# Turning the values of the looped head groups on VectorE instead of TensorE, and sharing out the closing sums

## The chip, the cores and the metric

The kernel runs on one core of a Trainium2 chip. The metric is the device time of one execution in microseconds, the median of several runs. Engine names are those of the profile: PE is TensorE (PEld its weight loads), DVE is VectorE, ACT is ScalarE, POOL is GpSimd, SP issues the DMAs.

## The reference

One decoder block on x of 8 sequences with 128 rows and 512 columns, in three residual steps:

```python
x = x + attn(layernorm(x))            # 32 query heads, 8 key/value heads of 128, causal softmax
x = x + cross(ctx, ctx, layernorm(x)) # sim = ctx @ query^T * scale, softmax, @ ctx
x = x + ffn(layernorm(x))             # 4-bit weights, 512 -> 1376 -> 512
...
q = (hidden_states @ w_q).reshape(B, S, Hkv, g, D)
k = (hidden_states @ w_k).reshape(B, S, Hkv, D)
v = (hidden_states @ w_v).reshape(B, S, Hkv, D)
...
attn = jnp.einsum('bhgqk,bkhd->bqhgd', probs, v)
return attn.reshape(B, S, Hq * D) @ w_o
...
inter = gate * jax.nn.sigmoid(gate) * up
out = (inter @ Wd).astype(jnp.float16)
```

## The kernel before

Most matmuls are done in three passes on numbers that are split into a high and a low part (`_hi`, `_lo`), so each product is `hi*hi + hi*lo + lo*hi` (`passes`, L495 to L498). ScalarE usually makes the high part by rounding, VectorE or GpSimd the low part by subtraction.

Self attention goes over 8 groups of heads (g), one key/value head with its 4 query heads each. Seven of them run in a hardware loop (`group(g)` of every engine), the eighth (`last_group`) is written out and mixed with the cross attention. A pass of the loop is cut into slots t; the work of every engine is written out slot by slot, and the engines meet only through semaphores. Sequence u (8 of them) has its scores in slot t = u (`scores`, L627), its mask, maximum and exponentials there too, the transposition of its probabilities (`turn_probs`, VectorE, ten blocks of 32x32 for 4 heads at once, L1413) in slot u + 1, the product with the values (`values(g, u)`, into one PSUM bank) in slot u + 2, the output projection (`out_heads(g, u)`) in slot u + 3, and its addition to the residual (`add_heads`, VectorE, L1403) in slot u + 4. Between them TensorE projects the next keys, values and queries: `FILL` says which of the 12 blocks (key, value, four query blocks, each for two halves of the batch) is projected in which slot, 12 matmuls each. The second half (n = 1) is that of this group, the first half (n = 0) that of the next group. ScalarE empties every block (`fill_out`, into `qt`, `kt` or `vt`).

The projected values come out with the head's 128 elements on the partitions, and `values` wants the keys there. So `turn_values` of TensorE transposes them in four pieces of 128x128 behind the first fill of slots 2 (n = 1) and 6 (n = 0) into the PSUM bank `BK_VT` (`turn_v`, L516); ScalarE rounds them there to `v_hi` (`values_first`, L837), VectorE subtracts to `v_lo` (`values_second`, L1373).

GpSimd has, for every sequence, the normalisation of the probabilities (L1164) and `pt_lo` (L1175), and the low parts of the weights (L1149). VectorE also unpacks 4-bit weights in four steps a pass (`unpack_step`, L1422 and L1427, in slots 0, 0, 9 and 10).

The feed forward part ends with eight products of the last row tile (`down_half`, two halves h of the rows, four column pieces j, each into a bank of its own). Piece j = 0 of each half is scaled by ScalarE (L1086) and added by GpSimd (L1246), pieces 1 to 3 are done by VectorE in one instruction (`last_sums`, L1639). TensorE transposes the sums of sequences 0 to 3, then 4 to 7 (L811); VectorE adds them to the residual (`last_adds`, L1646) but for those in `Y_POOL`, which ScalarE copies (L1090) and GpSimd adds (L1250); SP stores the 8 tiles in order (L485).

Of the kernel before, what the change touches and what calls it, by code (L numbers as in the profile page):

```python
# [17 lines left out]
P = 128  # L18
# [7 lines left out]
def decoder_kernel(nc, x, ctx_in, ctx_turned, w_q, w_k, w_v, w_o,  # L26
# [21 lines left out]
    TURN_V = {2: 1, 6: 0}  # L48
# [31 lines left out]
    with ExitStack() as stack:  # L80
# [56 lines left out]
        with ExitStack() as scope:  # L137
            sb = allocator(scope)
            xt_hi = sb("xt_hi", [P, HC, T], F32R)
            xt_lo = sb("xt_lo", [P, HC, T], F32R)  # L140
            wq_hi = sb("wq_hi", [P, HG, HC, P], F32R)
            wq_lo = sb("wq_lo", [P, HG, HC, P], F32R)
            wk_hi = sb("wk_hi", [P, HC, P], F32R)
            wk_lo = sb("wk_lo", [P, HC, P], F32R)
            wv_hi = sb("wv_hi", [P, HC, P], F32R)
            wv_lo = sb("wv_lo", [P, HC, P], F32R)
            wq_raw = sb("wq_raw", [P, HC, HG * P])
            wk_raw = sb("wk_raw", [P, HC, P])
            wv_raw = sb("wv_raw", [P, HC, P])
            wo_raw = sb("wo_raw", [P, HG, H])  # L150
            wo_hi = sb("wo_hi", [P, HG, H], F32R)
            wo_lo = sb("wo_lo", [P, HG, H], F32R)
            qt = sb("qt", [P, HG, T])
            kt = sb("kt", [P, T])
            vt = sb("vt", [P, HALF])
            v_hi = sb("v_hi", [P, NB, P], F32R)
            v_lo = sb("v_lo", [P, NB, P], F32R)
            probs = sb("probs", [P, 2, HG, P])
            pt = sb("pt", [P, HG, P])
            pt_hi = sb("pt_hi", [P, HG, P], F32R)  # L160
# [58 lines left out]
        vt_done = sem("vt_done")  # L219
        vt_hi = sem("vt_hi")  # L220
# [110 lines left out]
        Y_POOL = (2, 5)  # L331
# [158 lines left out]
        def _(pe):  # L490
# [23 lines left out]
            def turn_v():  # L514
                for k in range(BH):
                    mm = pe.transpose(psum[:, BK_VT, k * P:(k + 1) * P], vt[:, k * P:(k + 1) * P], ident[:])  # L516
# [48 lines left out]
            turn_v()  # L565
# [66 lines left out]
            def turn_values(g, n):  # L632
# [3 lines left out]
                turn_v()  # L636
# [180 lines left out]
        def _(act):  # L817
# [9 lines left out]
            def project_out(unit, n, bank):  # L827

                cols = slice(n * HALF, (n + 1) * HALF)
                dst = vt[:] if unit == "v" else kt[:, cols] if unit == "k" else qt[:, int(unit[1:]), cols]  # L830
# [92 lines left out]
            def values_first(g, n):  # L923

                act.wait_ge(vt_done, g * NH + (3 - n))
                act.wait_ge(pv_done, g * NB + (0 if n == 1 else BH) + PRIME)
                v_first(n)

            def fill_out(g, i):
# [3 lines left out]
                if unit == "v":  # L933
                    act.wait_ge(vt_done, g * NH + (2 - n))
# [24 lines left out]
            def group(g):  # L959
                step = g * NB  # L960
                for t in range(SLOTS):
                    if t < NB:
                        exponentials(g, t)
                    for k, i in enumerate(FILL.get(t, ())):
                        fill_out(g, i)
                        if k == 0 and t in TURN_V:
                            values_first(g, TURN_V[t])
# [115 lines left out]
            for h in range(NH):  # L1083
# [3 lines left out]
                        d_s[:, 0, NT - 1:NT]).then_inc(last_part, 1)  # L1087
            for i, b in enumerate(Y_POOL):
# [5 lines left out]
        def _(pool):  # L1094
# [73 lines left out]
            def group(g):  # L1168
                n = 0
                for t in range(SLOTS):  # L1170
# [71 lines left out]
            for h in range(NH):  # L1242
# [4 lines left out]
                                   ALU.add).then_inc(last_pool, 1)  # L1247
            for i, b in enumerate(Y_POOL):
# [5 lines left out]
        def _(dve):  # L1254
# [160 lines left out]

            def unpack_step(g, i):
# [60 lines left out]
            def group(g):  # L1477
                for t in range(SLOTS + 1):
# [12 lines left out]
                    if t in TURN_V:  # L1491
                        values_second(g, TURN_V[t])
# [4 lines left out]
                    if t in UNPACK:  # L1497
                        unpack_step(g, UNPACK[t])

# [150 lines left out]
            last_sums(1, (1,))  # L1650
            last_adds(0)
            last_sums(1, (2, 3))
# [38 lines left out]
```

## Time and profile before

| | |
|---|---|
| median of 3 runs | 733.5 us (733.18 to 734.48) |
| the profiled execution's own time | 734.44 us |
| its span | 732.5 us |
| TensorE busy | 713.0 us, 97% |
| VectorE busy | 563.0 us, 77% |
| ScalarE, GpSimd busy | 381.7 and 378.3 us, 52% each |
| TensorE clock granted over the span | 0.993 of full |
| DMA | 63.91 MB, 87 GB/s on average |

Busy time is the sum of the stretches in which an engine had an instruction. Matmuls are pipelined, and their ends are modelled: what one costs is read from the distance of the starts. Times in the rows below are us from the start of the span. One pass of the loop, from the scores of sequence 0 to the same in the next pass, takes some 68 us; the second of the seven goes from 99.7 to 167.7 us.

### The profile page before, as it was taken

To read this page: it belongs to the slowest core of one execution; us is meant where nothing else is said; L and a number is where in the kernel's file an instruction comes from. 1 tells how busy PE (TensorE), PEld (TensorE's weight loads), DVE (VectorE), ACT (ScalarE), POOL (GpSimd) and SP (SyncE) were. 2 spreads that over 40 slices of the span, in tenths; PEclk is the share of its full clock that TensorE was granted. 3 is DMA by queue.
4 is the path that set the end of the run, shared out by engine and by line. 5 is a ranking of instruction groups with operands and counts; after the bars stand their busy time and mean duration, and the time that the engine had idled before them with its cause. 6 is when DMAs were issued, how large, how long until landed. Compare 5 with 4: busy or idle time off the path is not lost.

```text
span 732.5 us, 11268 instructions
## 1 busy us (share of the span) xinstructions
PE 713.0 (97%) x3506; PEld 591.2 (81%) x3506; DVE 563.0 (77%) x1178; ACT 381.7 (52%) x965; POOL 378.3 (52%) x361
## 2 busy tenths in 40 slices
PE   8999999999999999999999999999999889999995
PEld 7888888888888888888888888888877657888873
DVE  6588768877886888688778867875378888888897
ACT  4575536535552654265346435652556556555552
POOL 4275426535542654264435525551445535788875
PEclk9999999999999999999999999999999999999997
DMA  9532046105701540361036003302900001321103
GB/s 303 163 84 91 2 125 210 38 0 144 230 0 38 175 152 0 97 190 38 0 115 200 0 9 99 142 0 73 334 10 2 0 4 55 86 82 41 30 12 115
DMA packets 44901, 63.91 MB, mean 87 GB/s; under 512 B 4462, under 2 KB 23278, under 8 KB 44878
## 3 DMA queue, kind: packets, MB, share of 16 engines
q1 hardware_dynamic: 44878, 63.62, 27.7%
q8 instruction: 12, 0.20, 0.1%
q14 instruction: 11, 0.09, 0.0%
HBM read 52.67 MB, written 10.95 MB: 87 GB/s over the span
## 4 chain that ended last, share of the span: by engine, by line
PE 87%; DVE 5%; POOL 3%; issue 2%; ACT 2%; DMA 0%; POOLq 0%; DVEq 0%; ACTq 0%
PE psum L496 21%; PE psum L498 21%; PE psum L497 21%; PE psum L627 7%; PE psum L715 5%; PE psum L716 5%; PE psum L738 2%; PE psum L737 2%; DVE stats L1267 1%; PE psum L516 1%; ACT probs L918 1%; PE psum L502 1%; POOL o_sum L1227 1%; DVE xprobs L1393 1%; DVE negmax L1458 0%
## 5 line engine op out<-in xcount | busy, mean ns | idle before, releaser
L1164 POOL TENSOR_TENSOR probs<-probs,rowinv 128x512 f32<-128x512 f32 x64 | 76.4, 1195 | 239.6 <-DVE rowinv L1464 239.6
L1413 DVE STREAM_TRANSPOSE pt<-probs 32x128 f32<-32x128 f32 x560 | 168.9, 302 | 13.9 <-POOL pt_lo L1175 7.1
L918 ACT ACTIVATE probs<-probs,negmax 128x128 f32<-128x128 f32 x256 | 99.8, 391 | 137.9 <-DVE negmax L1458 137.9
L496 PE MATMUL psum<-xt_hi,wq_hi 128*128 128x512 f32 x256 | 103.4, 404 | 0.0
L496 PE MATMUL psum<-wo_hi,at_hi 128*128 128x512 f32 x256 | 100.4, 392 | 0.5 <-DVE at_lo L1469 0.5
L498 PE MATMUL psum<-xt_hi,wq_lo 128*128 128x512 f32 x256 | 99.9, 390 | 0.0
L497 PE MATMUL psum<-xt_lo,wq_hi 128*128 128x512 f32 x256 | 99.8, 390 | 0.0
L498 PE MATMUL psum<-wo_hi,at_lo 128*128 128x512 f32 x256 | 99.7, 390 | 0.0
L497 PE MATMUL psum<-wo_lo,at_hi 128*128 128x512 f32 x256 | 99.6, 389 | 0.0
L1403 DVE TENSOR_TENSOR xacc<-psum,xacc 128x512 f32<-128x512 f32 x64 | 44.1, 690 | 64.5 <-PE psum L498 64.5
L1175 POOL TENSOR_TENSOR pt_lo<-pt,pt_hi 128x512 fp32r<-128x512 f32 x56 | 72.0, 1286 | 27.5 <-ACT pt_hi L974 27.5
L715 PE MATMUL psum<-ft_hi,gw 128*128 128x512 f32 (+1 forms) x176 | 71.2, 404 | 1.2 <-DVE ft_lo L1276 0.9
L627 PEld LDWEIGHTS psum<-kt,qt 128*128 128x128 f32 x512 | 66.8, 191 | 6.5 <-issue 1.4
L716 PE MATMUL psum<-ft_lo,gw 128*128 128x512 f32 (+1 forms) x176 | 69.7, 396 | 0.0
L832 ACT ACTIVATE qt<-psum 128x512 f32<-128x512 f32 x64 | 37.6, 588 | 59.6 <-PE psum L498 59.4
L627 PE MATMUL psum<-kt,qt 128*128 128x128 f32 x512 | 67.4, 274 | 0.3 <-ACT qt L832 0.3
L496 PEld LDWEIGHTS psum<-wo_hi,at_hi 128*128 128x128 f32 x256 | 48.1, 188 | 11.1 <-DVE at_lo L1469 1.2
L1454 DVE TENSOR_TENSOR probs<-psum,causal 128x512 f32<-128x512 f32 x64 | 44.2, 690 | 16.3 <-PE psum L627 16.1
L1469 DVE TENSOR_TENSOR at_lo<-psum,at_hi 128x512 fp32r<-128x512 f32 x64 | 43.2, 675 | 17.2 <-ACT at_hi L943 16.9
L498 PEld LDWEIGHTS psum<-xt_hi,wq_lo 128*128 128x128 f32 x256 | 48.0, 188 | 10.3
L498 PEld LDWEIGHTS psum<-wo_hi,at_lo 128*128 128x128 f32 x256 | 48.0, 188 | 10.2
L497 PEld LDWEIGHTS psum<-wo_lo,at_hi 128*128 128x128 f32 x256 | 48.1, 188 | 9.9
(153 smaller groups left out, 1530.8 us busy)
## 6 DMA issues: line engine op xcount, KB each, us to landing
wq_raw<-in_L_attn_w_q SPq DMA_DIRECT2D x8, 1024.0 KB, 5.6
wo_raw<-in_L_attn_w_o SPq DMA_DIRECT2D x8, 1024.0 KB, 7.8
u_zn<-zeros_gu SPq DMA_DIRECT2D x16, 344.0 KB, 6.4
unpacked_w<-u_q SPq DMA_DIRECT2D x8, 688.0 KB, 7.8
gw<-unpacked_w SPq DMA_DIRECT2D x20, 256.0 KB, 3.6
unpacked_w<-u_q SPq DMA_DIRECT2D x6, 512.0 KB, 6.7
u_q<-in_L_ffn_gate_qweight SPq DMA_DIRECT2D x8, 344.0 KB, 5.3
u_q<-in_L_ffn_up_qweight SPq DMA_DIRECT2D x8, 344.0 KB, 4.0
```

The source lines that it names most:

```text
L496: pe.matmul(dst, a_hi, b_hi, start=start, stop=False)
L497: pe.matmul(dst, a_hi, b_lo, start=False, stop=False)
L498: return pe.matmul(dst, a_lo, b_hi, start=False, stop=stop)
L627: mm = pe.matmul(psum[:, BK_S, j * P:(j + 1) * P], qt[:, j, t * P:(t + 1) * P], kt[:, t * P:(t + 1) * P], start=True, stop=True)
L715: pe.matmul(dst, gw[:, r, m, c, 0:w], ft_hi[:, c, cols], start=True, stop=False)
L716: return pe.matmul(dst, gw[:, r, m, c, 0:w], ft_lo[:, c, cols], start=False, stop=True)
L918: e = act.activation(probs[:, t % 2, j, :], probs[:, t % 2, j, :], ACT.Exp, bias=negmax[:, t % 2, j:j + 1], accum_out=rowsum[:, t % 2, j:j ...
L1164: pool.tensor_tensor(probs[:, t % 2], probs[:, t % 2], rowinv[:, t % 2, :].unsqueeze(2).to_broadcast([P, HG, P]), ALU.mult).then_inc(prob_ ...
L1175: pool.tensor_tensor(pt_lo[:], pt[:], pt_hi[:].bitcast(F32), ALU.subtract).then_inc(ptlo_ready, 1)
L1403: dve.tensor_tensor(xacc[:, u, :], psum[:, out_bank(g, u), :], xacc[:, u, :], ALU.add).then_inc(o_added, 1)
L1413: turned = dve.transpose(pt[keys, :, queries], probs[queries, t % 2, :, keys])
L1454: dve.tensor_tensor(probs[:, r], psum[:, BK_S, :].rearrange("p (a b) -> p a b", a=HG), causal[:].unsqueeze(1).to_broadcast([P, HG, P]), AL ...
```

## The change

The values of the looped groups are no longer transposed by TensorE. VectorE turns them in 16 blocks of 32 partitions for each half (`turn_values` there), one instruction for a block of four sequences, from `vt`, which now has a place for both halves, to a new tile `v_raw` in SBUF. `TURN_V` names the slots: half 1 in slots 1 to 4 with 4, 5, 4 and 3 blocks, half 0 in slots 8 to 10 with 4, 6 and 6. ScalarE rounds `v_raw` at the head of slots 5 and 11 (`values_rounded`), and the subtraction is now GpSimd's. The values ahead of the loop and those in the last group are turned as before.

In the closing part, the sum of piece 3 of the second half goes from VectorE to ScalarE and GpSimd; VectorE does its five sums ahead of all additions, and GpSimd's tiles are 3 and 6 in place of 2 and 5.

```diff
-    TURN_V = {2: 1, 6: 0}
+    TURN_V = {1: (1, 0, 4), 2: (1, 4, 9), 3: (1, 9, 13), 4: (1, 13, 16), 8: (0, 0, 4), 9: (0, 4, 10), 10: (0, 10, 16)}
+    SPLIT_V = {5: 1, 11: 0}
...
-            vt = sb("vt", [P, HALF])
+            vt = sb("vt", [P, 2, HALF])
+            v_raw = sb("v_raw", [P, BH, P])
...
-        Y_POOL = (2, 5)
+        Y_POOL = (3, 6)
...
# TensorE, group(g)
-                    for k, i in enumerate(FILL.get(t, ())):
+                    for i in FILL.get(t, ()):
                         fill(g, i)
-                        if k == 0 and t in TURN_V:
-                            turn_values(g, TURN_V[t])
...
             for b in range(NB):
-                pe.wait_ge(last_dve, (HC - 1) * (b // BH + 1))
-                pe.wait_ge(last_pool, b // BH + 1)
+                pe.wait_ge(last_dve, HC - 1 if b < BH else 2 * HC - 3)
+                pe.wait_ge(last_pool, 1 if b < BH else 3)
...
# ScalarE
+            def values_rounded(g, n):
+                act.wait_ge(v_turned, g * NH + (2 - n))
+                act.wait_ge(pv_done, g * NB + (0 if n == 1 else BH) + PRIME)
+                act.copy(v_hi[:, n * BH:(n + 1) * BH, :], v_raw[:]).then_inc(vt_hi, 1)
...
                 if unit == "v":
-                    act.wait_ge(vt_done, g * NH + (2 - n))
+                    act.wait_ge(vt_done, 1)
+                    act.wait_ge(v_turned, g * NH)
...
-                for t in range(SLOTS):
+                for t in range(SLOTS + 1):
+                    if t in SPLIT_V:
+                        values_rounded(g, SPLIT_V[t])
                     if t < NB:
                         exponentials(g, t)
...
+            act.wait_ge(last_done, NH * HC)
+            act.wait_ge(o_summed, SUMS_BEFORE + 2)
+            act.mul(o_part[:, 0, HALF:T], psum[:, NH * HC - 1, :], d_s[:, HC - 1, NT - 1:NT]).then_inc(last_part, 1)
...
# GpSimd
+                    if t in SPLIT_V:
+                        half = slice(SPLIT_V[t] * BH, (SPLIT_V[t] + 1) * BH)
+                        pool.wait_ge(vt_hi, g * NH + (3 - SPLIT_V[t]))
+                        pool.tensor_tensor(v_lo[:, half, :], v_raw[:], v_hi[:, half, :].bitcast(F32),
+                                           ALU.subtract).then_inc(vt_lo, 1)
...
+            pool.wait_ge(last_part, NH + 1)
+            done, count = copied(LAST_WINDOW, HC - 1)
+            pool.wait_ge(done, count)
+            pool.tensor_tensor(o16[:, HC - 1, HALF:T], o_part[:, 0, HALF:T], o_sum[:, HC - 1, HALF:T],
+                               ALU.add).then_inc(last_pool, 1)
...
# VectorE
+            def turn_values(g, n, first, last):
+                if first == 0:
+                    dve.wait_ge(proj_out, g * NBLK + FIRST_BLOCKS + BLOCKS.index(("v", n)) + 1)
+                    dve.wait_ge(vt_lo, g * NH + (2 - n))
+                for k in range(first, last):
+                    i, j = divmod(k, P // QUAD)
+                    heads, keys = slice(i * QUAD, (i + 1) * QUAD), slice(j * QUAD, (j + 1) * QUAD)
+                    turned = dve.transpose(v_raw[keys, :, heads],
+                                           vt[heads, n, :].rearrange("p (a b) -> p a b", a=BH)[:, :, keys])
+                if last == (P // QUAD) ** 2:
+                    turned.then_inc(v_turned, 1)
...
-                    if t in TURN_V:
-                        values_second(g, TURN_V[t])
                     if PV <= t < NB + 1:
                         heads_second(g, t - PV)
...
                     if t in UNPACK:
                         unpack_step(g, UNPACK[t])
+                    if t in TURN_V:
+                        turn_values(g, *TURN_V[t])
...
             last_sums(0, (1, 2, 3))
-            last_sums(1, (1,))
+            last_sums(1, (1, 2))
             last_adds(0)
-            last_sums(1, (2, 3))
             last_adds(1)
```

TensorE before, in slot 2: the end of its first fill, the four transposes of the values (`psum<-ident,vt`) and the start of the second fill.

```order
L497 MATMUL psum<-xt_lo,wq_hi 128x512
L498 MATMUL psum<-xt_hi,wq_lo 128x512
L635 ISA
L516 MATMUL psum<-ident,vt 128x128 x4
L643 REGISTER_ALU
L644 REGISTER_ALU
L496 MATMUL psum<-xt_hi,wq_hi 128x512
```

The same place in the changed kernel, whose lines are some three further down:

```order
L500 MATMUL psum<-xt_lo,wq_hi 128x512
L501 MATMUL psum<-xt_hi,wq_lo 128x512
L646 REGISTER_ALU
L647 REGISTER_ALU
L499 MATMUL psum<-xt_hi,wq_hi 128x512
```

The transposes and their wait are gone, and one block's matmuls follow the other's.

VectorE's row in slots 2 and 3 before, from mask(2) to the heads' subtraction of sequence 1 (`probs<-psum,causal` is the mask, `negmax` the maximum, `rowinv` the reciprocal, `at_lo` the subtraction of the heads, `v_lo` that of the values):

```order
L1454 TENSOR_TENSOR probs<-psum,causal 128x512
L1458 TENSOR_REDUCE negmax<-probs 128x4
L1413 STREAM_TRANSPOSE pt<-probs 32x4x32 x10
L1464 RECIPROCAL rowinv<-rowsum 128x4
L1474 ISA
L1373 TENSOR_TENSOR v_lo<-psum,v_hi 128x512
L1469 TENSOR_TENSOR at_lo<-psum,at_hi 128x512
L1453 REGISTER_ALU
L1454 TENSOR_TENSOR probs<-psum,causal 128x512
L1458 TENSOR_REDUCE negmax<-probs 128x4
L1413 STREAM_TRANSPOSE pt<-probs 32x4x32 x10
L1464 RECIPROCAL rowinv<-rowsum 128x4
```

The same place now, with the reciprocal of slot 1 and the first four blocks ahead of it:

```order
L1498 RECIPROCAL rowinv<-rowsum 128x4
L1440 ISA
L1441 ISA
L1445 STREAM_TRANSPOSE v_raw<-vt 32x4x32 x4
L1487 REGISTER_ALU
L1488 TENSOR_TENSOR probs<-psum,causal 128x512
L1492 TENSOR_REDUCE negmax<-probs 128x4
L1434 STREAM_TRANSPOSE pt<-probs 32x4x32 x10
L1498 RECIPROCAL rowinv<-rowsum 128x4
L1503 TENSOR_TENSOR at_lo<-psum,at_hi 128x512
L1445 STREAM_TRANSPOSE v_raw<-vt 32x4x32 x5
L1487 REGISTER_ALU
```

The subtraction of the values has left, and 4 and 5 block transposes stand at the ends of slots 1 and 2, ahead of the next slot's mask.

VectorE's last rows before:

```order
L1639 SCALAR_TENSOR_TENSOR o<-psum,d_s,o_sum 128x512 x4
L1646 TENSOR_TENSOR xacc<-psum,xacc 128x512 x3
L1639 SCALAR_TENSOR_TENSOR o<-psum,d_s,o_sum 128x512 x2
L1646 TENSOR_TENSOR xacc<-psum,xacc 128x512 x3
```

And now:

```order
L1673 SCALAR_TENSOR_TENSOR o<-psum,d_s,o_sum 128x512 x5
L1680 TENSOR_TENSOR xacc<-psum,xacc 128x512 x6
```

One sum has left, and none stands behind an addition any more.

## Rows read from the trace of the kernel before

**Rows 1.** The page: span, and busy time of each engine.
```profile
span 732.5 us, 11268 instructions
...
PE 713.0 (97%) x3506; PEld 591.2 (81%) x3506; DVE 563.0 (77%) x1178; ACT 381.7 (52%) x965; POOL 378.3 (52%) x361
```

**Rows 2.** Windows: second pass; length, busy PE, PEld, DVE, ACT, POOL, granted clock, DMA.
```profile
99.70:167.70 68.00, 68.00 (x337) 57.45 (x336) 52.40 (x126) 34.46 (x104) 32.27 (x26) 1.00 0.34 100
```

**Rows 3.** Waits of TensorE, whole span: us in total, times, longest.
```profile
PE psum L496 <- DVE at_lo L1469: 0.5, 1, 0.5
...
PE psum L627 <- ACT qt L832: 0.3, 1, 0.3
```

**Rows 4.** Timeline of TensorE, second pass: start, us, line, operation; score blocks, transposes.
```profile
103.28 1.05 PE L627 MATMUL psum<-kt,qt 128*128 128x128 f32 x8
...
109.63 1.05 PE L627 MATMUL psum<-kt,qt 128*128 128x128 f32 x8
...
113.26 0.60 PE L516 MATMUL psum<-ident,vt 128*128 128x128 f32 x4
...
117.12 1.05 PE L627 MATMUL psum<-kt,qt 128*128 128x128 f32 x8
...
131.18 1.05 PE L627 MATMUL psum<-kt,qt 128*128 128x128 f32 x8
...
138.20 1.05 PE L627 MATMUL psum<-kt,qt 128*128 128x128 f32 x8
...
145.72 0.49 PE L627 MATMUL psum<-kt,qt 128*128 128x128 f32 x3
```

**Rows 5.** Timeline of VectorE, slots 2 to 5; in brackets the idle time before.
```profile
112.74 3.14 DVE L1413 STREAM_TRANSPOSE pt<-probs 32x128 f32<-32x128 f32 x10 [0.61 <-POOL pt_lo L1175]
...
116.01 0.66 DVE L1373 TENSOR_TENSOR v_lo<-psum,v_hi 128x512 fp32r<-128x512 f32 x1
117.94 0.69 DVE L1469 TENSOR_TENSOR at_lo<-psum,at_hi 128x512 fp32r<-128x512 f32 x1 [1.27 <-ACT at_hi L943]
118.55 0.68 DVE L1454 TENSOR_TENSOR probs<-psum,causal 128x512 f32<-128x512 f32 x1
...
124.35 0.69 DVE L1403 TENSOR_TENSOR xacc<-psum,xacc 128x512 f32<-128x512 f32 x1 [0.51 <-PE psum L498]
125.24 0.69 DVE L1454 TENSOR_TENSOR probs<-psum,causal 128x512 f32<-128x512 f32 x1 [0.20 <-PE psum L627]
...
131.38 0.69 DVE L1403 TENSOR_TENSOR xacc<-psum,xacc 128x512 f32<-128x512 f32 x1 [0.88 <-PE psum L498]
```

**Rows 6.** Timeline of GpSimd, second pass: normalisation, weight splits, pt_lo.
```profile
104.14 2.44 POOL L1164 TENSOR_TENSOR probs<-probs,rowinv 128x512 f32<-128x512 f32 x1 [13.06 <-DVE rowinv L1464]
106.54 2.54 POOL L1149 TENSOR_TENSOR wo_lo<-wo_raw,wo_hi 128x512 fp32r<-128x512 f32 x2
...
131.00 1.27 POOL L1175 TENSOR_TENSOR pt_lo<-pt,pt_hi 128x512 fp32r<-128x512 f32 x1
```

**Rows 7.** Timeline of the closing part, all engines, from 719 us.
```profile
719.35 2.72 DVE L1639 SCALAR_TENSOR_TENSOR o<-psum,d_s,o_sum 128x512 f16<-128x512 f32 x4
...
720.55 2.49 POOL L1246 TENSOR_TENSOR o<-o_part,o_sum 128x512 f16<-128x512 f32 x2
...
721.96 1.48 PE L811 MATMUL psum<-ident,o 128*128 128x128 f16 x16 [1.28 <-POOL o L1246]
...
723.10 6.88 SPq L485 DMA_DIRECT2D out<-xacc  x8
...
725.64 1.89 PE L811 MATMUL psum<-ident,o 128*128 128x128 f16 x16 [2.20 <-DVE o L1639]
...
727.38 1.26 POOL L1250 TENSOR_TENSOR xacc<-y_part,xacc 128x512 f32<-128x512 f32 x1 [2.39 <-ACT y_part L1090]
```

**Rows 8.** Windows: slots 8 to 10 of the second pass, columns as in rows 2.
```profile
157.84:168.60 10.76, 10.76 (x54) 9.05 (x52) 5.11 (x6) 1.19 (x2) 1.28 (x1) 1.00 0.20 29
```

**Rows 9.** Windows: 730 to 731 us, columns as in rows 2, last the GB/s.
```profile
730.00:731.00 1.00, 0.00 (x0) 0.00 (x0) 0.00 (x0) 0.00 (x0) 0.00 (x0) 0.50 1.03 383
```

More of the change, by code:

```diff
@@ L219, in decoder_kernel @@
         vt_done = sem("vt_done")
+        v_turned = sem("v_turned")
         vt_hi = sem("vt_hi")
@@ L512, in project, with turn_v @@
                 mm.then_inc(proj_done, 1)
-            def turn_v():
+            def turn_v(n):
                 for k in range(BH):
-                    mm = pe.transpose(psum[:, BK_VT, k * P:(k + 1) * P], vt[:, k * P:(k + 1) * P], ident[:])
+                    mm = pe.transpose(psum[:, BK_VT, k * P:(k + 1) * P], vt[:, n, k * P:(k + 1) * P], ident[:])
                 mm.then_inc(vt_done, 1)
@@ L564, in _ @@
             pe.wait_ge(ln_lo[0], NB)
-            turn_v()
+            turn_v(0)
             def out_heads(g, u):
@@ L635, in turn_values @@
                 pe.wait_ge(vt_lo, g * NH + (2 - n))
-                turn_v()
+                turn_v(n)
             def fill(g, i):
@@ L829, in project_out @@
                 cols = slice(n * HALF, (n + 1) * HALF)
-                dst = vt[:] if unit == "v" else kt[:, cols] if unit == "k" else qt[:, int(unit[1:]), cols]
+                dst = vt[:, n] if unit == "v" else kt[:, cols] if unit == "k" else qt[:, int(unit[1:]), cols]
                 if unit[0] == "q":
@@ L923, in values_first @@
             def values_first(g, n):
-                act.wait_ge(vt_done, g * NH + (3 - n))
+                act.wait_ge(vt_done, 3 - n)
                 act.wait_ge(pv_done, g * NB + (0 if n == 1 else BH) + PRIME)
                 v_first(n)
+            def values_rounded(g, n):
+                act.wait_ge(v_turned, g * NH + (2 - n))
+                act.wait_ge(pv_done, g * NB + (0 if n == 1 else BH) + PRIME)
+                act.copy(v_hi[:, n * BH:(n + 1) * BH, :], v_raw[:]).then_inc(vt_hi, 1)
             def fill_out(g, i):
@@ L960, in group @@
                 step = g * NB
-                for t in range(SLOTS):
+                for t in range(SLOTS + 1):
+                    if t in SPLIT_V:
+                        values_rounded(g, SPLIT_V[t])
                     if t < NB:
                         exponentials(g, t)
-                    for k, i in enumerate(FILL.get(t, ())):
+                    for i in FILL.get(t, ()):
                         fill_out(g, i)
-                        if k == 0 and t in TURN_V:
-                            values_first(g, TURN_V[t])
                     if PV <= t < NB + PV:
@@ L1169, in group @@
                 n = 0
-                for t in range(SLOTS):
+                for t in range(SLOTS + 1):
+                    if t in SPLIT_V:
[3 more added lines that the diff above has]
+                                           ALU.subtract).then_inc(vt_lo, 1)
                     if t < NB:
```

## The prediction

> **What bounds the kernel now.** I read the page first. TensorE is busy 713.0 of 732.5 us and the next engine, VectorE, 563.0 [rows 1]. A share near the whole does not prove a bound, because matmul spans overlap, so I took one stretch as long as one pass of the loop over head groups: TensorE is busy all 68.00 us at full granted clock, while VectorE has work for 52.40, ScalarE for 34.46 and GpSimd for 32.27 [rows 2]. The list of TensorE's waits has only two short ones that name attention operands, 0.5 and 0.3 us, once each [rows 3]; asked for 33 to 507 us alone, the view lists none. So in the seven passes every TensorE instruction has its price in the time, and work on other engines has none until it makes TensorE wait.
>
> The timeline of TensorE gives the prices [rows 4]. A slot runs from one score block to the next. Slot 1 (scores, 24 matmuls) lasts 109.63 - 103.28 = 6.35. Slots 3 and 4 (scores, 27 matmuls each) last (131.18 - 117.12) / 2 = 7.03, so a 512 column matmul costs 0.68 / 3 = 0.227, and scores with 12 of them 6.35 - 12 x 0.227 = 3.62. Slots 2 and 6 have the same 27 matmuls and the four transposes of the values: 117.12 - 109.63 = 7.49 and 145.72 - 138.20 = 7.52.
>
> **The change in the loop: TensorE.** Without the transposes these two slots should last as long as slots 3 and 4: 0.46 + 0.49 = 0.95 a pass, 7 passes: **6.65 us**. The profiler's length of the four, 0.60 [rows 4], is not their price, since neighbours overlap; it would give 14 x 0.60 = 8.4 as the upper bound. The four transposes ahead of the loop and four in the last group stay.
>
> **The loop: VectorE.** It loses two subtractions a pass, 2 x 0.6 (0.66 long at 116.01, less the overlap with what follows), and gains 32 block transposes. The trace has none from vt, but ten from probs of the same shape, strides and alternating quadrants, taking 3.14 [rows 5]: 0.314 each. The bounds of the unknown: 0.31 below, since nothing in it is smaller than in the like instruction, and 0.66 above (the subtraction over four times the partitions [rows 5]); I take 0.314. A pass then asks VectorE for 52.4 - 1.2 + 10.0 = 61.2 of 67.1 us. It fits as a sum, so the question is the place.
>
> I walk the slots on the time axis of before, with TensorE 0.46 earlier from slot 3 on:
> - Slot 1: four transposes, 1.26. They push mask(2) and turn_probs(1), which had idled 0.61 for GpSimd; the rest of at most 0.65 ends in the 1.27 that the heads' subtraction idled [rows 5].
> - Slot 2: the heads' subtraction comes at 117.94 - 0.46 = 117.48, five transposes (1.57) follow, and mask(3) starts at 119.66 and not at 118.55: 1.1 late.
> - Slot 3: four more (1.26) on top. add_heads(0) had idled 0.51 and mask(4) 0.20 more (its start is 0.89 behind, where VectorE's own pace is 0.61); the lateness is 1.8 at the first, 1.5 at the second.
> - Slot 4: three more (0.94), less the 0.88 that add_heads(1) had idled and 0.28 at mask(5): 1.2 late.
> - Slot 5: none; another 0.88 of idle time, as in slot 4, and 0.28 bring it to about 0, and the subtraction gone from slot 6 does the rest.
>
> What is queued behind: turn_probs, then ScalarE's pt_hi, GpSimd's normalisation and pt_lo, and for pt_lo TensorE's values(u). values(3) stands in slot 5 behind scores and 12 matmuls: 131.18 + 3.62 = 134.80, now 134.34. Its pt_lo started at 131.00 [rows 6]; with 1.5 it starts at 132.5, ends at 133.77 and with 0.14 of handing over (GpSimd's first closing addition ends 721.82, TensorE starts 721.96 [rows 7]) is there at 133.9. **Spare: 0.43 us**. The same sum for values(2) leaves 0.5 and for values(4) 0.7. ScalarE, whose exponentials are 1.1 late in slot 3, has about as little room for the last query block, which scores(4) needs. No wait, then, but little room: the nine transposes of slots 2 and 3 make up the 1.5, so from 0.314 + 0.43/9 = 0.36 each on, TensorE waits.
>
> Slots 8 to 10 take 4, 6 and 6. VectorE idled 10.76 - 5.11 = 5.65 us there [rows 8], in gaps in front of add_heads(5), (6) and (7), and 16 x 0.314 = 5.0 fits; only add_heads(6) slips, by 0.6, and nobody waits for it, since its bank is used again in the next pass. The second half therefore costs nothing; if that cover were gone, out_heads(7) would wait.
>
> ScalarE's rounding now reads SBUF at the head of slots 5 and 11, ahead of exponentials that it waits for anyway. GpSimd gets two subtractions a pass, 2 x 1.27 [rows 6], with 32.3 of 68 us busy: the one of slot 5 lies between its weight split and a normalisation 3 us off, the one of slot 11 has two slots until values(0). Price 0. SP's queue and the DMAs keep their order and their triggers.
>
> **The same pair by a rule.** Four 128x128 turns cost TensorE 0.48 and would cost VectorE 16 x 0.314 = 5.0 [rows 4, 5]: ten times the engine time, given to an engine that has it free. The Trainium skill ("VectorE: DVE Perf Modes", Rules for kernel authors) says of a 128x128 transpose: "Use TensorE if PSUM dest is OK", which it was. By that rule the change is wrong, as it is if VectorE has no room; by the rows it has, and that rule's case is the slower rival below.
>
> **The closing part.** Before, TensorE's second set of transposes starts at 725.64, behind VectorE's last two sums, which stood behind its additions of the first half [rows 7]. Now VectorE does five sums in a row (719.35 + 2.72 + 0.68 = 722.75) and ScalarE and GpSimd the last. ScalarE's product lies under GpSimd's pair, which runs to 720.55 + 2.49 = 723.04; a third addition ends at 724.27, so TensorE can start at **724.4, 1.2 earlier**. GpSimd's output tile is now the third turned of its half and not the second: it started 1.74 behind TensorE, now 1.74 + 0.43, so it ends at 724.4 + 2.17 + 1.26 = 727.8 instead of 728.64: 0.8. Two stores stand from there on in SP's queue and not three. A store costs 0.45 in the queue (three from 728.64 to 729.98) or 0.68 by the rate at which they drain (256 KB at 383 GB/s [rows 9]). Sum 1.25 to 1.5; I take **1.4**. Bounds: 0, if what GpSimd gives back is lost again, and 1.5.
>
> **Sum.** 6.65 + 1.4 = 8.05 us. The profiled execution took 734.44 us, 1.94 more than its span; its like would be 726.4. It stands 0.94 above the median of the three runs, 733.5, so the median should be **725.4 us**.
>
> **Rivals.**
> - *The closing part gives nothing.* The critical engine there becomes GpSimd, at 1.25 an addition against VectorE's 0.69. For it: it then has three sums and two tiles in a row. Against: the starts above. Time 733.5 - 6.65 = 726.8. Chance 0.07.
> - *GpSimd is slowed beside the new transposes.* The first normalisation of a pass, beside VectorE's unpacking, takes 2.44 where others take 1.04. If those of slots 2 to 4 did too, pt_lo would be 1.4 later and values(2) or values(3) would wait about 1.4 - 0.43 = 0.97 a pass: 7 x 0.97 = 6.8, time 732.2. Against: the two splits at 106.54, wholly beside ten transposes, take 1.27 each, like any other [rows 6]. The Trainium skill ("GPSIMD Engine Reference", 1. Specifications) names the SBUF interface that GpSimd shares with VectorE, and contention with instructions of two SBUF inputs or in a 2-port mode. Our 2.44 lies beside one with two inputs and agrees; a transpose has one. Chance 0.10, of which 0.07 for a part of it that still ends faster.
> - *Slower: VectorE becomes the bound.* Place: slots 2 to 4. If a transpose from vt costs c, values(3) waits 9 (c - 0.314) - 0.43; this eats the 0.95 from c = 0.47 on. At c = 0.66 VectorE alone needs 52.4 - 1.2 + 21.1 = 72.3 us a pass against 68.05 now: 7 x 4.25 - 1.4 makes at least 762. For it: the small spare, and each hand-over that I took too short. Against: the like instructions [rows 5]. Chance 0.07.
> - *The removal is no gain,* because the four transposes lie in a gap that another wait would fill: 733. Against: no wait is there [rows 3]. Chance 0.04.
>
> **Chances and range.** The forecast has 0.72. A difference under 0.2%, 1.5 us, can hardly be told from none here. Faster: 0.72 + 0.07 + 0.07 = 0.86; same 0.03 + 0.04 = 0.07; slower 0.07. The forecast's own range is 724.6 (0.50 for every set, closing 1.5, 0.4 of spread between runs) to 726.8. To leave out no more than 0.2 it goes up into the second rival: 724.5 to 729.0.
>
> **What would show it.** A pass of the loop 67.1 us long, with slots 2 and 6 at 7.03; no TensorE wait in it; ten and 4, 5, 4, 3 transposes at 0.31; mask(4) some 1.5 us later behind its scores; pt_lo at 1.28 and normalisations at 1.04 in slots 2 to 4; TensorE's last transposes 1.2 us sooner behind the last matmul. Waits of values(2), (3) or (4) for pt_lo, or of scores(4) for ScalarE's qt, would make it wrong, as would block transposes above 0.36.

## The result, and the profile after

The changed kernel took 724.79 us (median of 4 runs, 724.76 to 725.17); the kernel before, beside it on the same chip, 733.34 (733.1 to 734.48). The ratio is 0.9883, with a 95% interval from 0.9871 to 0.9894: 8.55 us less, where 8.05 and a time of 725.4 were forecast.

The page of the changed kernel, its span and its engines' busy time, answers to [rows 1]:
```profile
span 723.0 us, 11410 instructions
...
PE 705.2 (98%) x3450; PEld 586.2 (81%) x3450; DVE 617.4 (85%) x1387; ACT 384.8 (53%) x966; POOL 397.9 (55%) x376
```
TensorE has 56 instructions less, 14 sets of four; VectorE 224 - 14 - 1 = 209 more, and 54 us more of work. The windows of the second pass and of two stretches of the closing part (length, busy PE, PEld, DVE, ACT, POOL, granted clock, DMA, GB/s) answer to [rows 2]:
```profile
98.90:165.99 67.09, 67.09 (x329) 56.70 (x328) 60.27 (x156) 34.77 (x105) 34.87 (x28) 1.00 0.33 102
...
714.00:716.00 2.00, 1.81 (x16) 1.54 (x16) 2.00 (x5) 0.16 (x1) 2.00 (x2) 0.50 0.00 0
...
717.00:718.00 1.00, 0.91 (x12) 0.73 (x10) 0.98 (x2) 0.28 (x1) 0.78 (x1) 0.81 1.03 385
```
A pass lasts 67.09 us and TensorE is busy all of it; VectorE has 60.27 and not 52.40. The timeline of TensorE, second pass, gives the slots, as [rows 4] did:
```profile
102.53 1.05 PE L630 MATMUL psum<-kt,qt 128*128 128x128 f32 x8
108.87 1.05 PE L630 MATMUL psum<-kt,qt 128*128 128x128 f32 x8
115.90 1.05 PE L630 MATMUL psum<-kt,qt 128*128 128x128 f32 x8
122.93 1.05 PE L630 MATMUL psum<-kt,qt 128*128 128x128 f32 x8
129.95 1.05 PE L630 MATMUL psum<-kt,qt 128*128 128x128 f32 x8
136.98 1.05 PE L630 MATMUL psum<-kt,qt 128*128 128x128 f32 x8
144.01 1.05 PE L630 MATMUL psum<-kt,qt 128*128 128x128 f32 x8
```
Slot 2 is 115.90 - 108.87 = 7.03 and slot 6 144.01 - 136.98 = 7.03; before they were 7.49 and 7.52. Slot 1 is still 6.34. The view of waits lists none of TensorE inside the loop.

VectorE's timeline, slots 1 to 4, against [rows 5]:
```profile
109.43 1.22 DVE L1445 STREAM_TRANSPOSE v_raw<-vt 32x128 f32<-32x128 f32 x4
...
111.98 3.15 DVE L1434 STREAM_TRANSPOSE pt<-probs 32x128 f32<-32x128 f32 x10
...
117.44 1.56 DVE L1445 STREAM_TRANSPOSE v_raw<-vt 32x128 f32<-32x128 f32 x5
119.02 0.69 DVE L1488 TENSOR_TENSOR probs<-psum,causal 128x512 f32<-128x512 f32 x1
...
124.30 1.25 DVE L1445 STREAM_TRANSPOSE v_raw<-vt 32x128 f32<-32x128 f32 x4
...
126.17 0.68 DVE L1488 TENSOR_TENSOR probs<-psum,causal 128x512 f32<-128x512 f32 x1
...
131.44 0.95 DVE L1445 STREAM_TRANSPOSE v_raw<-vt 32x128 f32<-32x128 f32 x3
```
The transposes of vt run like those of probs: 1.22, 1.56 and 0.95 for 4, 5 and 3, so 0.31 each. mask(4) starts at 126.17, 3.24 behind its scores at 122.93; before, 1.09 behind. Of the 2.15 between, 0.46 is TensorE being earlier and 1.69 VectorE being later. GpSimd's timeline in the same slots, against [rows 6]:
```profile
123.77 1.04 POOL L1175 TENSOR_TENSOR probs<-probs,rowinv 128x512 f32<-128x512 f32 x1 [3.94 <-DVE rowinv L1498]
124.77 1.29 POOL L1191 TENSOR_TENSOR pt_lo<-pt,pt_hi 128x512 fp32r<-128x512 f32 x1
...
131.91 1.30 POOL L1191 TENSOR_TENSOR pt_lo<-pt,pt_hi 128x512 fp32r<-128x512 f32 x1
```
pt_lo at 124.77 lies beside the four transposes of 124.30 and takes 1.29, no longer than elsewhere. The closing part, all engines, against [rows 7]:
```profile
711.33 3.38 DVE L1673 SCALAR_TENSOR_TENSOR o<-psum,d_s,o_sum 128x512 f16<-128x512 f32 x5
...
712.28 0.40 PE L739 MATMUL psum<-int_lo,dw 96*128 96x512 f32 x1
712.52 2.50 POOL L1262 TENSOR_TENSOR o<-o_part,o_sum 128x512 f16<-128x512 f32 x2
...
713.94 1.86 PE L812 MATMUL psum<-ident,o 128*128 128x128 f16 x16 [1.26 <-POOL o L1262]
...
714.98 1.28 POOL L1267 TENSOR_TENSOR o<-o_part,o_sum 128x512 f16<-128x512 f32 x1
...
716.40 1.51 PE L812 MATMUL psum<-ident,o 128*128 128x128 f16 x16 [0.60 <-POOL o L1267]
716.50 1.27 POOL L1271 TENSOR_TENSOR xacc<-y_part,xacc 128x512 f32<-128x512 f32 x1 [0.25 <-ACT y_part L1101]
...
718.39 1.26 POOL L1271 TENSOR_TENSOR xacc<-y_part,xacc 128x512 f32<-128x512 f32 x1 [0.61 <-ACT y_part L1101]
```
The last matmul of the down projection ends at 712.68. The second set of transposes starts 3.72 behind it (before 725.64 - 720.68 = 4.96), GpSimd ends 6.97 behind it (before 7.96), the span 10.32 behind it (before 11.82). GpSimd's two output tiles are tile 3, ready at 716.50 + 1.27 = 717.77, and tile 6, ready at 719.65. The stores do not run in one piece. What the DMA queue moved from 714 to 723 us, in 40 slices of equal length:
```profile
GB/s 0 0 0 0 0 0 0 0 0 109 391 391 373 391 382 382 392 382 291 9 118 382 400 364 382 410 364 382 364 392 392 373 392 382 373 337 18 0 0 0
```
Up to the dip lie three stores of 256 KB, behind it five. The fourth is that of tile 3, so the queue waited for GpSimd.

The spans differ by 9.5 us, the medians by 8.55. The part between the last head group and the closing part, with its feed-forward matmuls, is the same in both kernels. It lasted 132.54 us in the profiled execution of before and 131.01 in that of the changed kernel. This 1.5 goes with the execution and not with the change: e2 below, which has the loop of before, had 130.93, and e12, which has a loop of the changed kind, 132.50.

### The profile page after: what moved, and what is told of

It is laid out like the page before. It is cut to its first block, busy times and chain, and to the rows that moved or that the text cites. A ratio compares the mean times of both kernels' runs of the same rounds, so it can differ in the third digit from the quotient of the medians.

```text
span 723.0 us, 11410 instructions
## 1 busy us (share of the span) xinstructions
PE 705.2 (98%) x3450; PEld 586.2 (81%) x3450; DVE 617.4 (85%) x1387; ACT 384.8 (53%) x966; POOL 397.9 (55%) x376
## 4 chain that ended last, share of the span: by engine, by line
PE 88%; DVE 5%; POOL 2%; ACT 2%; issue 2%; POOLq 0%; DVEq 0%; ACTq 0%
PE psum L500 21%; PE psum L499 21%; PE psum L501 21%; PE psum L630 8%; PE psum L716 5%; PE psum L717 5%; PE psum L739 2%; PE psum L738 2%; PE psum L526 1%; DVE stats L1288 1%; ACT probs L919 1%; PE psum L505 1%; POOL o_sum L1243 1%; DVE xprobs L1414 1%; DVE negmax L1492 0%
## 5 line engine op out<-in xcount | busy, mean ns | idle before, releaser
L1445 DVE STREAM_TRANSPOSE v_raw<-vt 32x128 f32<-32x128 f32 x224 | 67.5, 301 | 3.5
L501 PEld LDWEIGHTS psum<-xt_hi,wq_lo 128*128 128x128 f32 x256 | 48.1, 188 | 10.1
L951 ACT CAST at_hi<-psum 128x512 fp32r<-128x512 f32 x64 | 37.1, 579 | 35.6 <-PE psum L501 34.3
```

What stands on the lines that cost most here:

```text
L501: return pe.matmul(dst, a_lo, b_hi, start=False, stop=stop)
L1445: turned = dve.transpose(v_raw[keys, :, heads], vt[heads, n, :].rearrange("p (a b) -> p a b", a=BH)[:, :, keys])
```

## The experiments

All are built on the changed kernel unless said otherwise. Prices of a pass are read from the traces, since the medians of one kernel on two occasions differ by some tenths of a us.

**e1_loop_only** and **e2_closing_only** part the two halves of the change. e1 has the closing part of before, e2 is the kernel before with the changed closing part, whose core is:
```diff
-            last_sums(1, (1,))
+            last_sums(1, (1, 2))
             last_adds(0)
-            last_sums(1, (2, 3))
             last_adds(1)
```


> The changed loop with the closing part of before. Theory (two parts that add up, the loop 6.7 and the closing part 1.5 us): 726.3 us, with 11.8 us from the end of the last down matmul to the end, as in the kernel before, and loop passes of 67.1 us. Rival (the closing part gave nothing, all 8.5 us come from the loop and what follows it): 724.8 us.

> The kernel before with the changed closing part alone. Theory: 731.8 us, 1.5 less than before, and 10.3 us from the last down matmul's end to the end. Rival (the closing part gives nothing): 733.3 us. Its feed forward part is word for word that of both kernels, so its distance from matmul to matmul there also tells whether the 0.233 us of before and the 0.230 of after belong to the kernels or to the execution.

e1: 726.14 us, ratio 0.9898 (0.9883 to 0.9913); a pass 67.09, the second set of transposes 4.98 behind the last matmul, the end 11.4 behind it. e2: 731.48, ratio 0.9972 (0.9962 to 0.9982); a pass 68.05, the second set 3.73 behind, the end 10.24 behind. So the loop gives all of its 0.96 a pass alone, and the closing part 1.1 (changed kernel against e1) to 1.6 (e2 against before) alone; the medians say 1.35 and, against 733.6 for before on that occasion, 2.1.

**e3_idle_turns** gives TensorE four useless transposes in slots 2 and 6 and leaves everything else.
```diff
+            def idle_turns():
+                for k in range(BH):
+                    pe.transpose(psum[:, BK_VT, k * P:(k + 1) * P], causal[:], ident[:])
...
+                        if k == 0 and t in (2, 6):
+                            idle_turns()
```


> The changed kernel, in which TensorE does four 128x128 transposes of a constant in slots 2 and 6 besides; nobody reads them. Theory (TensorE's time is the price, 0.48 us a set, 14 sets): 6.7 us more than the changed kernel, 731.5 us, passes of 68.05 us. Rival (the gain came from the work that ScalarE and VectorE lost, or from a wait on the values): 724.8 us, as the changed kernel.

732.83 us, ratio 0.9995 (0.9985 to 1.0005), passes 68.05: four transposes that nobody reads cost exactly what the removed ones gave. The 1.3 above the expected 731.5 lie ahead of the loop, in a wait of 1.74 us that the experiment itself had to add for the bank that the useless transposes write. In the timeline of TensorE:
```profile
33.35 0.82 PE L630 MATMUL psum<-kt,qt 128*128 128x128 f32 x5 [1.74 <-DVE v_lo L1401]
```

**e4_crowded** keeps the 16 blocks of the second half and all their work, and moves them out of slot 1.
```diff
-    TURN_V = {1: (1, 0, 4), 2: (1, 4, 9), 3: (1, 9, 13), 4: (1, 13, 16), 8: ...
+    TURN_V = {2: (1, 0, 6), 3: (1, 6, 12), 4: (1, 12, 16), 8: ...
```


> The changed kernel with the 16 block transposes of half 1 as 0, 6, 6 and 4 in slots 1 to 4 in place of 4, 5, 4 and 3: the same work, one slot more crowded. Theory (the place decides, by the walk of the prediction): mask(3) 1.4 us late, after slot 3 another 1.88 less 0.79, so 2.4 to 2.5 late; values(3) then waits 2.45 - 1.5 - 0.43 = 0.5 us for pt_lo in each pass, 3.6 us in all: 728.4 us. Rival (only VectorE's sum of 61 of 67 us counts): 724.8 us, no wait.

731.87 us, ratio 0.9983 (0.9973 to 0.9993). A pass of 68.06: the whole gain of the loop is gone, twice what was expected. TensorE around values(3):
```profile
134.15 0.39 PE L501 MATMUL psum<-xt_hi,wv_lo 128*128 128x512 f32 x1
134.87 0.50 PE L499 MATMUL psum<-pt_hi,v_hi 128*128 128x512 f32 x1 [0.33 <-POOL pt_lo L1191]
135.20 0.39 PE L500 MATMUL psum<-pt_lo,v_hi 128*128 128x512 f32 x1
```
Matmuls start 0.227 apart when nothing disturbs them. Here the first comes 0.72 behind its neighbour, so 0.49 late where 0.5 was expected. Two errors cancel in this: pt_lo came 0.83 later than in the changed kernel and not 0.95, and the room for it was 0.32 up to this matmul and not 0.43 (worked out below). The next matmul comes 0.33 behind and not 0.227, and values(4), which I had not counted, was late by 0.2 and again by such a tenth. The 0.33 in brackets is less than the 0.49 lost, since the tail of the previous matmul covers 0.16 of it: the sum in the view of waits (2.3 us for seven passes) hides two thirds of what these waits cost.

**e5_twice** makes VectorE transpose every block twice, first into a spare tile.
```diff
-                    turned = dve.transpose(v_raw[keys, :, heads],
-                                           vt[heads, n, :].rearrange("p (a b) -> p a b", a=BH)[:, :, keys])
+                    for dst in (v_spare, v_raw):
+                        turned = dve.transpose(dst[keys, :, heads],
+                                               vt[heads, n, :].rearrange("p (a b) -> p a b", a=BH)[:, :, keys])
```


> The changed kernel, in which VectorE does each block transpose of the values twice, the first time to a tile that nobody reads: 64 a pass, as if one cost 0.63 us. Theory (VectorE becomes the bound, the slower rival of the prediction): it then has 51.2 + 20.1 = 71.3 us of work a pass, and more than that in time, since it idles for TensorE in slots 0 and 6 to 8; passes of 72 to 74 us, so 724.8 + 7 x (5 to 7) = 760 to 773 us, slower than the kernel before. Rival (waits do not add up, only the one of values(3), 9 x 0.314 - 0.43 = 2.4 us a pass): 741.6 us.

750.14 us, ratio 1.0221 (1.0205 to 1.0236): slower than before, but neither the 760 to 773 of the theory nor the 741.6 of its rival. The first pass lasts 70.2 us and the others 70.6, where 72 to 74 were expected. VectorE did not become the bound by its sum: it is busy for 66.2 us of such a pass. The edit also gave it less work than I had counted, since from one block to the next there are 0.51 us and not 0.63 (the second transposition of a block is recorded with 0.26). With a cost of 0.51 the formula of the slower rival, 9 (c - 0.314) - 0.43, makes 1.3 us a pass at values(3) alone; measured are 3.5. The waits of TensorE, in total, times, longest:
```profile
PE psum L500 <- POOL pt_lo L1192: 5.2, 14, 0.4
PE psum L631 <- ACT qt L834: 4.6, 8, 0.7
PE psum L500 <- DVE at_lo L1505: 4.6, 8, 0.6
```
They name three engines, at more places than values(3). The edit adds work to VectorE alone, so ScalarE and GpSimd pass its lateness on. So the slower rival's place is real, and its price at one place too low.

**e10_one_more**, **e11_even** and **e12_two_more** change only how many blocks stand in slots 1 to 4: 3, 5, 5, 3, then 4, 4, 4, 4, then 3, 6, 5, 2. With the changed kernel (nine in slots 2 and 3) and e4 (twelve) they make a row: eight, nine, ten, eleven, twelve.
```diff
-    TURN_V = {1: (1, 0, 4), 2: (1, 4, 9), 3: (1, 9, 13), 4: (1, 13, 16), 8: ...
+    TURN_V = {1: (1, 0, 3), 2: (1, 3, 8), 3: (1, 8, 13), 4: (1, 13, 16), 8: ...
```


> The changed kernel with the blocks of the second half spread 3, 5, 5, 3 over slots 1 to 4 instead of 4, 5, 4, 3: values(3) is reached one block transpose (0.31 us) later against a spare of 0.31 to 0.36. Theory (a threshold with no other loss): 0 to 0.1 us a pass, no change, 724.8 to 725.5. If each interruption of the matmul stream costs 0.1 beside the wait itself, as e4_crowded suggests, and the spare is missed: 0.1 to 0.2 a pass, 725.5 to 726.2.

> The changed kernel with the blocks spread 4, 4, 4, 4. Compared with 4, 5, 4, 3: mask(3) comes one block transpose (0.31 us) earlier and what stands in slot 4 (the last batch, then ScalarE's v_hi and GpSimd's v_lo of that half) about where it did. Theory (spare on VectorE is worth nothing): 724.8, passes 67.09, no wait of TensorE. Rival (the long last batch makes v_lo late for values of slot 5 or 6): a wait in slot 5 or 6 and over 725.5.

e11: 725.1 us, ratio 0.9891 (0.9876 to 0.9906), passes 67.09: spare time of VectorE is worth nothing. e10: 725.77, ratio 0.9902 (0.9888 to 0.9917), and a pass of 67.24, 0.15 more, although the first matmul of values(3) is on time. The weight loads of TensorE show why. First the changed kernel:
```profile
133.13 0.19 PEld L501 LDWEIGHTS psum<-xt_hi,wv_lo 128*128 128x128 f32 x1
133.35 0.19 PEld L499 LDWEIGHTS psum<-pt_hi,v_hi 128*128 128x128 f32 x1
```
then e10, its loads and its matmuls:
```profile
133.18 0.19 PEld L501 LDWEIGHTS psum<-xt_hi,wv_lo 128*128 128x128 f32 x1
133.63 0.19 PEld L499 LDWEIGHTS psum<-pt_hi,v_hi 128*128 128x128 f32 x1 [0.26 <-POOL pt_lo L1191]
133.74 0.19 PEld L500 LDWEIGHTS psum<-pt_lo,v_hi 128*128 128x128 f32 x1
```
```profile
133.41 0.39 PE L501 MATMUL psum<-xt_hi,wv_lo 128*128 128x512 f32 x1
133.64 0.50 PE L499 MATMUL psum<-pt_hi,v_hi 128*128 128x512 f32 x1
133.97 0.40 PE L500 MATMUL psum<-pt_lo,v_hi 128*128 128x512 f32 x1
```
A weight load normally starts with the matmul ahead of its own, 0.23 early, and here it is the load that waits for pt_lo. It does so because the kernel has this wait in front of the whole product (`values`). The load brings v_hi for the matmul with pt_hi; only the second matmul reads pt_lo. (A wait placed one matmul later might give back 0.23; no run tried it.) In the changed kernel pt_lo ended at 131.91 + 1.30 = 133.21 and the load was due at 133.35. In e10 the load came 0.22 late, just in time for its matmul; what suffered was the next one, 0.33 behind. Counted at the load, the price at values(3) is its lateness less 0.12: 0.10 here and 0.60 for e4's 0.72. The other 0.05 of e10's pass lie in the matmuls just behind and in slot 6. The next run tests this price:

> The changed kernel with the blocks of the second half spread 3, 6, 5, 2 over slots 1 to 4: eleven in slots 2 and 3, where the changed kernel has nine, e10_one_more ten and e4_crowded twelve. Theory: the operand pt_lo is asked for by the weight load that runs one matmul ahead, 0.23 us before its matmul. In the changed kernel that load had 0.09 us of spare; in e10_one_more it was 0.22 late and a pass cost 0.15 more; in e4_crowded 0.72 late and values(3) cost about 0.60. So the price is the load's lateness less 0.12. Here the load should be 0.09 + 0.31 = 0.53 late counted from e10_one_more's 0.22, the matmul 0.30 late, the price of values(3) 0.41 us a pass; values(4) not late, since three blocks fewer than in e4_crowded stand ahead of it. Passes 67.5 (67.45 to 67.6), seven passes 2.9 us, median 727.7 us. Rival (only the idle time that the view of waits shows is lost, 0.16 less than the matmul's lateness): 0.15 a pass, 725.8. Rival (a missed turn costs a whole 0.5 or more, as in e4_crowded, wherever it comes): 728.3 or more.

728.75 us, ratio 0.9927 (0.9911 to 0.9943), passes of 67.55 to 67.59. TensorE's loads at scores(4) and around values(3), and its timeline, slots 3 to 5:
```profile
123.47 0.97 PEld L630 LDWEIGHTS psum<-kt,qt 128*128 128x128 f32 x8 [0.30 <-ACT qt L833]
...
133.80 0.19 PEld L501 LDWEIGHTS psum<-xt_hi,wv_lo 128*128 128x128 f32 x1
134.41 0.19 PEld L499 LDWEIGHTS psum<-pt_hi,v_hi 128*128 128x128 f32 x1 [0.42 <-POOL pt_lo L1191]
```
```profile
116.41 1.05 PE L630 MATMUL psum<-kt,qt 128*128 128x128 f32 x8
...
123.47 1.16 PE L630 MATMUL psum<-kt,qt 128*128 128x128 f32 x8
...
130.63 1.05 PE L630 MATMUL psum<-kt,qt 128*128 128x128 f32 x8
...
134.41 0.50 PE L499 MATMUL psum<-pt_hi,v_hi 128*128 128x512 f32 x1
134.75 0.39 PE L500 MATMUL psum<-pt_lo,v_hi 128*128 128x512 f32 x1
...
137.95 1.05 PE L630 MATMUL psum<-kt,qt 128*128 128x128 f32 x8
```
The load for values(3) was due at 134.02 and 0.39 late, not 0.53: TensorE itself came 0.16 later, which the expectation had not counted. Its slot lasts 7.32, and by its own start-to-start distances values(3) lost 0.16 + 0.11 = 0.27, which is 0.39 - 0.12. The 0.16 arose before: the scores at 123.47 take 1.16 and not 1.05, slot 3 lasts 7.06 and slot 4 7.16. Their load waited for ScalarE's qt (123.42 was its end), and it does so in every pass: this is the place that the prediction had named beside values(3). So a pass falls in the expected 67.45 to 67.6 partly by other terms than expected. Neither wait stands in the view of TensorE's matmuls, which is empty for this loop; the same view for its weight loads lists 2.8 us for pt_lo and 2.1 for qt. The median is 3.96 above the changed kernel and 1.0 above the forecast; the seven passes explain 3.3. Its six executions fall in two groups, 727.5 to 727.9 and 729.6 to 730.1, and in the profiled one, of the slower group, the part between took 132.5, as in that of before. Both rivals are out by the trace: 0.15 or a whole 0.5 at values(3) isn't there.

**e6_last_half** and **e8_last_gaps** extend the change to the last group, whose second half TensorE still turns. e6 puts eight blocks behind the heads' subtraction of slots 1 and 2 each, e8 ten ahead of it in slot 1 and six behind it in slot 2. The core of e8's edit on VectorE:
```diff
+    LAST_TURNS = {1: (0, 10), 2: (10, 16)}
...
+                    if t == 1:
+                        turn_values(LAST, 1, *LAST_TURNS[t])
                     if t >= 1:
                         heads_second(LAST, t - 1)
+                    if t == 2:
+                        turn_values(LAST, 1, *LAST_TURNS[t])
```


> The changed kernel with the last group's second half of the values turned by VectorE too, eight blocks at the end of slot 1 and eight of slot 2 there, rounded by ScalarE and subtracted by GpSimd at the head of slot 3. Theory (TensorE bounds the last group as well at that place, VectorE idles 3.0, 1.1 and 3.3 us there): one set of transposes less, 0.48 us: 724.3 us. Rival (the group's chain through VectorE, ScalarE and GpSimd is tighter than the loop's, 2.5 us more of VectorE in a slot delays the mask): 724.8 us or more.

> As e6_last_half, but VectorE's block transposes lie where VectorE idles: ten ahead of at_lo of slot 1 (idle there 3.26 us, and the 0.69 of v_lo leaves VectorE), six behind at_lo of slot 2 (idle 2.37). Theory (only the place in VectorE's row cost in e6): mask and pt_lo of slot 2 start where they do in the changed kernel, TensorE saves its four transposes once, 0.48 us: the last group 79.3 us where the changed kernel has 79.8 and e6 had 82.0; median 724.3. Rival (the longer way of the values, by block transposes, ScalarE's v_hi and GpSimd's v_lo in slot 3, is itself what costs): still above 726.

e6: 727.36 us, ratio 0.9911 (0.9897 to 0.9924), slower than the changed kernel and 3.1 above the theory. The last group takes 82.02 where that has 79.81. VectorE and TensorE in e6:
```profile
517.34 2.50 DVE L1448 STREAM_TRANSPOSE v_raw<-vt 32x128 f32<-32x128 f32 x8
519.85 0.69 DVE L1491 TENSOR_TENSOR probs<-psum,causal 128x512 f32<-128x512 f32 x1
```
```profile
521.92 0.50 PE L500 MATMUL psum<-pt_hi,v_hi 128*128 128x512 f32 x1 [1.74 <-DVE pt_lo L1546]
```
Here VectorE itself makes pt_lo, and the eight transposes stood ahead of mask(2), which had no idle time in front of it. e8: 724.61, ratio 0.9881 (0.9866 to 0.9896), last group 79.35: the same 16 transposes, in VectorE's gaps of 3.26 and 2.37 us, give the 0.46 that four transposes of TensorE cost. Against the changed kernel this is 0.06%, too little for the medians to tell; that it is faster rests on the last group in the trace, and the expected 724.3 was missed by 0.3.

**e7_six_sums** and **e9_early_adds** ask what ends the kernel. In e7 VectorE does all six closing sums in a row, with no third one for ScalarE and GpSimd; e9 is e8 with two additions ahead of the fifth sum. The core of e9's edit:
```diff
-            last_sums(1, (1, 2))
-            last_adds(0)
-            last_adds(1)
+            last_sums(1, (1,))
+            last_adds(0, (0, 1))
+            last_sums(1, (2,))
+            last_adds(0, (2, 3))
+            last_adds(1)
```


> The changed kernel, but VectorE does all six closing sums in a row and the additional sum by ScalarE and GpSimd is gone. Theory A (the start of TensorE's second set of transposes decides): VectorE's sixth sum ends 0.68 after its fifth, 715.4 in the time of the changed kernel's trace, so the second set starts at 715.6 and not at 716.40, and the kernel ends 0.8 us earlier: 724.0 us. Theory B (the stores decide: eight of 256 KB at 385 GB/s are 5.45 us, and the first becomes ready 0.7 us later, behind the sixth sum): no gain, 724.8 to 725.2 us.

> e8_last_gaps, and in the closing part VectorE does the first two additions ahead of its fifth sum. GpSimd's third sum ends last for the second set of transposes (0.60 us of wait on it), so the fifth sum may end some 0.5 later. Theory (the eight stores, 0.69 us each, back to back, set the end): the first store starts about 0.3 us earlier and so does the end: 0.2 to 0.3 us below e8_last_gaps if the third store isn't late; its own addition comes 0.2 later and leaves about no spare. Rival (the second set of transposes sets the end): no change, or 0.1 to 0.3 slower by a later fifth sum.

e7: 726.22 us, ratio 0.9894 (0.9878 to 0.991), above both theories (724.0, and 724.8 to 725.2). Its second set of transposes starts 2.8 behind the last matmul, 1.0 earlier than in the changed kernel, and its end is 10.59 behind, against 10.32: theory A is out, and the stores of theory B set the end. Only this 0.27 of the 1.1 us by which its span is longer belongs to the closing part; the rest lies ahead of the loop and in the part between. e9: 724.91, ratio 0.9888 (0.9872 to 0.9903), not the 0.2 to 0.3 below e8's 724.61 that were expected: its end is 10.35 behind, e8's 10.01. The GB/s of the closing part in slices of equal length, e7 from 714 to 724:
```profile
GB/s 0 0 0 0 0 0 0 0 0 0 0 0 0 0 82 393 369 385 393 385 377 393 361 377 393 377 385 393 352 401 393 369 401 385 369 377 279 0 0 0
```
and e9 from 714 to 723:
```profile
GB/s 0 0 0 0 0 0 0 0 27 355 382 373 383 391 364 55 0 328 364 373 364 373 419 346 400 400 355 400 364 173 364 382 382 373 400 364 64 0 0 0
```
e7's stores run without a gap: with 256 KB at some 383 GB/s each, they set its end from the first store on. e9's first store began earlier, but after two of them the queue ran dry for half a us: the third store's addition now stands behind the fifth sum. (e8 and e9 also differ in the granted clock of their transposes, 1.00 and 0.50 for most of the time, so the 0.34 between them is not the order's alone.) The two orders tried each move the dry place and gain nothing.

## Why the prediction was right

- **The bound.** TensorE's instructions had their price: 0.96 a pass against 0.95, 6.7 us against 6.65. e3 takes it back by adding nothing but TensorE work.
- **VectorE.** The forecast of 0.314 held (0.31 in a row, 0.301 as the mean of the 224 records), and within 1 us the busy time: 60.27 a pass, 61.2 forecast. mask(4) was 1.69 late and not 1.5, as each batch costs about a tenth beside its transposes.
- **The spare at values(3) is the step that was wrong.** I put 0.43, with a hand-over of 0.14 from GpSimd to TensorE, seen in the closing part, and counted to the matmul. The spare was 0.09. The load that waits for pt_lo is asked for 0.23 earlier than the matmul. pt_lo started 1.67 later in its pass and not 1.5, and took 1.30 and not 1.27. Against these three stands a shorter hand-over: such a load started 0.05 behind the end of pt_lo (e10: 133.58, 133.63). So 0.43 - 0.23 - 0.17 - 0.03 + 0.09 = 0.09, and from the rows 133.35 - 133.21 - 0.05 = 0.09. The change came through with less than a third of one block transpose to go; that it lost nothing there is partly luck. So the threshold that the slower rival needed was nearer than 0.47 a transpose, and the chance of 0.07 for it was held up by like instructions being alike, not by the spare. The sign that would have shown it, waits of values(3) and of scores(4), was the right one: e10 has the first, e12 both.
- **GpSimd beside transposes.** pt_lo 1.29, normalisations 1.04: that rival is out. The Trainium skill ("GPSIMD Engine Reference", 1. Specifications) ties contention to two SBUF inputs or a 2-port mode; the trace agrees, in that a transpose with its one input slowed nothing here.
- **The rule for transposes.** Moving them gave 0.96 a pass while it cost VectorE ten times the engine time. The Trainium skill ("VectorE: DVE Perf Modes", Rules for kernel authors) would leave them on TensorE. The measurement decides against it for this kernel; e4 and e5 show that it is right again where the transposes stand in the wrong slots (nothing gained) or where VectorE has 66.2 of 70.6 us to do (16 us slower than before).
- **The closing part.** 1.4 forecast; 1.50 by the traces of the two kernels, 1.1 to 1.6 with e1 and e2. Compared at a granted clock near 1.00 in both sets of transposes (e1: sets of 1.05 and 1.11 us, end 11.39 behind the last matmul; e4: 1.05 and 1.05, end 9.97 behind) it is 1.42. The second set came 1.24 earlier (1.2 forecast), GpSimd ended 0.99 earlier (0.8). The path to the end was only half right. In these traces the end can be counted from a tile that the store queue waits for: 0.68 for each store from there on, and 1.8 behind them. Before, that tile was GpSimd's second: 7.96 + 3 x 0.68 + 1.8 = 11.8, from which the 1.8 is taken. For the changed kernel I had followed GpSimd's second tile again, number 6: 6.97 + 2 x 0.68 + 1.8 = 10.1. But its first, number 3, which now stands behind its third sum, was ready 5.09 behind the last matmul with five stores to come: 5.09 + 5 x 0.68 + 1.8 = 10.3, and 10.32 was measured. The later of the two counts fits the traces of e2, e3, e4, e6, e8 and e10 within 0.1 as well; in e2, e3, e6 and e10 it is that of tile 6. So the two paths lie within 0.3 of each other, and that 1.4 came out although the other one set the end is partly luck.
- **The other rivals.** The closing part gave its gain (e1, e2), and the passes of 67.09, with e3, rule out that the removal was none.

## What to carry to other kernels

When one engine is busy through the whole loop, work moved off it pays in full, even to an engine that needs ten times as long, as long as it lies in that engine's idle time: ask first where the idle time is, in front of which instruction, and who waits for what comes behind. In the last group the same 16 transposes gave 0.46 us or cost 2.2 by their place alone, and in the loop the place of 16 of them decided whether a pass gained 0.96 or nothing. Count a spare of TensorE to the weight load that runs one matmul ahead, if the wait stands in front of it. Read a loss from the distance between starts and from the waits of the weight loads, not from the waits of the matmuls.

## What was not expected of the hardware

- In e10 the weight load of values(3) was 0.22 us late. Its matmul started on time, and the one behind it 0.33 later and not 0.227: a wait that no row of a matmul shows cost 0.1 us. Four cases agree with the load's lateness less 0.12: 0.22, 0.39 in e12, 0.39 at values(4) of e4 (0.28 lost), and 0.72. A load that was 0.08 late (values(4) of e10) cost 0.01.
- The sixteen f16 transposes of a set in the closing part took 1.05 to 1.89 us in different executions. In the changed kernel the granted clock was 0.50, its lower level of 1.2 GHz, from 714 to 717 us, with 1.86 for the first set and 1.51 for the second; 0.81 from 717 to 718; and 1.00, or 2.4 GHz, from 718 to 720. TensorE had stood idle from 712.68 to 713.94 just before. In e8 it was idle as long (712.89 to 714.14), the clock stayed at 1.00 through both sets, and each took 1.05. A part of the differences between closing parts is this.
- Matmuls in the middle of the part between stood 0.229 us apart on average in the changed kernel's profiled execution and 0.233 in those of before and of e12, with a granted clock of 1.00 in all three; the code is the same there. This moves the time by 1.5 us, and what decides it is open.
